# Layer norm, causal attention and a gated expert block: expert product in two pieces, four buffers for h, and another rule for the first score visits

## The chip, the cores and the metric

The kernel runs on one core of one Trainium2 chip. The metric is the device time of one execution in microseconds (us); less is better. Five engines work beside each other: TensorE (PE in the rows, its weight loads PEld), VectorE (DVE), ScalarE (ACT), GpSimd (POOL) and SyncE (SP), which here only issues DMAs. Each engine runs its own list of instructions in order and waits on semaphores for the others.

## The reference

For each of 8 sequences of 512 tokens with 128 channels (everything float32):

```
x = x + attn(layernorm(x))     # 16 heads of 8 channels, causal softmax, w_qkv, w_proj
x = x + experts(layernorm(x))

def experts(x):                # x: tokens x 128
    p = sigmoid(x @ Wg + bg)                      # 8 gates for each token
    weights = p * (p > 0.5)
    h = relu(einsum('td,edh->eth', x, W1) + b1)   # 8 experts, 512 hidden
    y = einsum('eth,ehd->etd', h, W2) + b2
    return einsum('te,etd->td', weights, y)
```

`layernorm` takes off the mean and multiplies by 1/sqrt(variance + 1e-5), without a scale or an offset.

## The kernel before

**Tiling.** A sequence lies with its 128 channels on the partitions and its 512 tokens along the row. The hidden layer of all experts is 4096 wide, which gives 32 slots of 128 for a sequence, four for each expert. A product of float32 accuracy is made of three matmuls in a faster form, from a high and a low part of each operand: `z` (slot s of x·W1) is L1107 to L1109, `y` (slot s of h·W2, added up in `y_bank` over the four slots of an expert) is L1293, L1295 and L1297. Between them ScalarE makes `h_hi` with a relu (L863), and the low part `h_lo` is made by VectorE straight from the bank (L1070, 20 slots of 32) or by GpSimd from a copy `h_all` (L869, L762, 12 slots). `h_hi` and `h_lo` are rings of three buffers. VectorE multiplies a finished expert by its gate (`term`, L1083), GpSimd adds it up (`acc`, L772). The gates are computed once for a sequence, written to memory (`gout`, L662) and read back, spread over all partitions, by one DMA for each expert (`wb`, L669) into four buffers.

**Attention.** Four groups of four heads. For a group there are 10 "max" units (scores with queries on the partitions; VectorE takes the row maxima, `smax`, L1018) and 10 "ex" units (scores with keys on the partitions and the maximum already taken off; ScalarE takes the exponential, L831). The scores come from `stack`, which holds the high and low parts of q and k interleaved: three DMAs for a group from `parts` (L641), and a fourth inside `stack` (L644). The maxima go GpSimd, TensorE (`nm`, L1238), ScalarE (L819) and SyncE (`mrow`, L655: two DMAs) back into `stack`. A *visit* of TensorE (L1166, with the causal mask added by L1178 for max units) takes two max units, or two ex units, or two of each side by side. GpSimd zeroes what is masked (`causal`, L755), and `pv` (L1248, 32 matmuls) multiplies by v.

**Layer norm.** VectorE takes statistics (L901, L905), GpSimd makes rstd (L713, L716), and VectorE normalises with four `tensor_scalar` instructions of 128x128 (L910), for `xT` (first norm) and `x2T` (second norm). Both write the buffer `xn`.

**What sets the order.** `list_schedule` makes the list of every engine before the program is built. Every item (`put` in `work_items`) has a due time, a cost in ns and the items it waits for; `SHIFT` moves the due times of a kind, for the first sequence (True) and for the others (False). An engine that falls idle takes the ready item with the earliest due time. `visits()` fixes the pairs of the score visits beforehand: the ex units follow the max units at a lag of 18 units until unit 50, and 12 from then on. TensorE has seven banks (`ring`), and `y_bank` as an eighth until the second norm of the first sequence (`EARLY_RING`). As long as there are eight, TensorE issues a dummy matmul (`warm`, L1193, result unused) when something is ready and cannot start. The item `("pe", ("y", i, s))` waits for `h_lo` of its slot; its first two matmuls read only `h_hi`.

**The start.** SyncE issues the loads of x, W1, the small weights and the third x, then the stack DMAs. The load of the third x (L630) waits for `x_bp` (GpSimd, L723), and this for the last of the small loads. VectorE first clears `stack` (L878, L879) and `nm` (L880). In the trace the masks are made at 3.1 us, the first transposes of TensorE start at 10.3, its matmuls on the small weights end at 18.35, and the first visit starts at 23.12.

## Time and profile before

| | |
|---|---|
| three runs | 685.42, 686.25, 686.25 us (median 686.25) |
| the profiled execution | 686.17 us, of it a span of 684.4 us |
| TensorE busy | 650.2 us, 95% of the span |
| VectorE, ScalarE, GpSimd busy | 480.8, 418.6, 330.9 us (70, 61, 48%) |
| mean granted clock of TensorE | 0.989 of full speed |
| by slices of 17.1 us, TensorE | 2 tenths, then 7, then 9 to the last slice (6) |

The span is what lies between the first and the last instruction of the profile; 1.8 us of the execution lie around it. A matmul is counted as busy until its result has landed, and the next starts before that; so the time that a matmul costs is read from the starts of two neighbours.

### The profile page before, as it was taken

How to read it: one execution, taken by the hardware profiler on the slowest of the kernel's cores; microseconds unless marked ns; L12 is line 12 of the kernel's file. 1: busy time of each engine (PE TensorE's matmuls, PEld its weight loads, DVE VectorE, ACT ScalarE, POOL GpSimd, SP SyncE). 2: the span in 40 equal slices, each digit the busy share in tenths (PEclk: the TensorE clock that was granted, in tenths of full speed). 3: DMA queues.
4: the chain of work that ended last, by engine and by line, in shares of the span. 5: the costliest groups of instructions: out<-in, count | busy, mean ns of one | idle time of the engine just before them, and what ended most of it. 6: DMA issues, size and time to landing. Idle time of an engine off the chain costs nothing.

```text
span 684.4 us, 13158 instructions
## 1 busy us (share of the span) xinstructions
PE 650.2 (95%) x4486; PEld 449.4 (66%) x4486; DVE 480.8 (70%) x958; ACT 418.6 (61%) x793; POOL 330.9 (48%) x409
## 2 busy tenths in 40 slices
PE   2799999999999989999999989999999999999996
PEld 2355666667666766667666756667666766677774
DVE  5797687679876796669866696668866676546443
ACT  2158656667666666676666566666666666665553
POOL 4018434556435454556335555455245564545554
PEclk9799999999999999999999999999999999999998
DMA  6442213210322113210222113220222102100310
GB/s 191 111 125 52 51 42 104 57 42 17 87 73 57 41 26 108 69 42 18 86 63 54 40 39 106 57 56 3 59 87 57 42 2 80 48 17 6 103 32 16
DMA packets 29954, 40.44 MB, mean 59 GB/s; under 512 B 4064, under 2 KB 14184, under 8 KB 29888
## 3 DMA queue, kind: packets, MB, share of 16 engines
q1 hardware_dynamic: 29360, 39.40, 21.4%
q8 instruction: 37, 0.61, 0.3%
q10 hardware_dynamic: 528, 0.20, 0.1%
q14 instruction: 29, 0.24, 0.1%
HBM read 23.72 MB, written 2.23 MB: 38 GB/s over the span
## 4 chain that ended last, share of the span: by engine, by line
PE 85%; DVE 6%; issue 3%; DMA 2%; SPq 2%; POOL 1%; ACT 1%; POOLq 0%; DVEq 0%
PE ring L1166 11%; PE ring L1248 10%; PE ring L1107 9%; PE ring L1109 9%; PE ring L1108 9%; PE y_bank L1293 8%; PE y_bank L1297 8%; PE y_bank L1295 8%; PE ring L1178 6%; PE ring L1113 3%; DVE xn L910 2%; PE ring L1193 2%; DVE negmax L1018 1%; DMA g_w<-in_L_ffn_b 1%; PE ring L1228 1%
## 5 line engine op out<-in xcount | busy, mean ns | idle before, releaser
L863 ACT ACTIVATE h_hi<-ring 128x512 fp32r<-128x512 f32 x256 | 153.4, 599 | 126.2 <-PE ring L1109 110.2
L831 ACT ACTIVATE pt<-ring 128x512 f32<-128x512 f32 x313 | 172.0, 596 | 54.7 <-PE ring L1166 51.8
L762 POOL TENSOR_TENSOR h_lo<-h_all,h_hi 128x512 fp32r<-128x512 f32 x96 | 123.9, 1290 | 149.5 <-ACT h_all L869 149.0
L1018 DVE TENSOR_REDUCE negmax<-ring 128x1 f32<-128x512 f32 (+1 forms) x185 | 119.2, 683 | 74.3 <-PE ring L1178 74.2
L1070 DVE SCALAR_TENSOR_TENSOR h_lo<-ring,h_hi 128x512 fp32r<-128x512 f32 x160 | 109.5, 686 | 56.0 <-ACT h_hi L863 52.7
L755 POOL TENSOR_SCALAR_AFFINE_SELECT pt<-pt 128x512 f32<-128x512 f32 x128 | 80.1, 640 | 110.9 <-ACT pt L831 110.8
L1293 PE MATMUL y_bank<-h_hi,w_lo 128*128 128x512 f32 x256 | 109.0, 426 | 1.1 <-DVE f_buf L1083 0.5
L1107 PE MATMUL ring<-x2T_lo,w_hi 128*128 128x512 f32 x256 | 108.0, 422 | 0.3 <-DVE negmax L1018 0.3
L1166 PE MATMUL ring<-stack 32*128 32x256 f32 (+3 forms) x992 | 94.9, 363 | 8.7 <-DMA stack<-stack 4.8
L1297 PE MATMUL y_bank<-h_lo,w_hi 128*128 128x512 f32 x256 | 100.6, 393 | 0.0
L1109 PE MATMUL ring<-x2T_hi,w_hi 128*128 128x512 f32 x256 | 100.5, 393 | 0.0
L1295 PE MATMUL y_bank<-h_hi,w_hi 128*128 128x512 f32 x256 | 99.9, 390 | 0.0
L1108 PE MATMUL ring<-x2T_hi,w_lo 128*128 128x512 f32 x256 | 99.9, 390 | 0.0
L1166 PEld LDWEIGHTS ring<-stack 32*128 32x128 f32 x992 | 55.4, 183 | 61.3 <-issue 55.3
L1018 DVE TENSOR_REDUCE pm<-ring 128x4 f32<-128x512 f32 x123 | 80.7, 681 | 13.0 <-PE ring L1178 12.2
L772 POOL TENSOR_TENSOR f_buf<-f_buf 128x512 f32<-128x512 f32 x56 | 72.2, 1290 | 21.2 <-DVE f_buf L1083 21.2
L1248 PE MATMUL ring<-pt,v_sb 128*32 128x512 f32 (+3 forms) x1024 | 75.5, 436 | 0.0
L1083 DVE SCALAR_TENSOR_TENSOR f_buf<-y_bank,b_cols,f_buf 128x512 f32<-128x512 f32 x64 | 47.9, 748 | 21.5 <-PE y_bank L1297 21.3
L1248 PEld LDWEIGHTS ring<-pt,v_sb 128*32 128x32 f32 x1024 | 30.0, 109 | 47.7 <-issue 42.1
L869 ACT ACTIVATE h_all<-ring 128x512 f32<-128x512 f32 x96 | 56.9, 592 | 0.0
L1293 PEld LDWEIGHTS y_bank<-h_hi,w_lo 128*128 128x128 f32 x256 | 48.2, 188 | 11.9 <-issue 2.0
L1178 PE MATMUL ring<-mask,ident 128*128 128x128 bf16 (+1 forms) x308 | 55.3, 258 | 0.0
(119 smaller groups left out, 754.1 us busy)
## 6 DMA issues: line engine op xcount, KB each, us to landing
f_buf<-gates SPq DMA_DIRECT2D x64, 256.0 KB, 3.3
stack<-parts SPq DMA_DIRECT2D x96, 128.0 KB
x_in<-in_L_attn_x SPq DMA_DIRECT2D x8, 256.0 KB, 2.9
f_buf<-in_L_ffn_W SPq DMA_DIRECT2D x1, 2048.0 KB, 10.4
out_x<-f_buf SPq DMA_DIRECT2D x8, 256.0 KB, 2.3
stack<-nmT SPq DMA_DIRECT2D x64, 8.0 KB
stack<-stack SPq DMA_DIRECT2D x32, 16.0 KB
bv<-in_L_attn_b_qkv SPq DMA_DIRECT2D x1, 256.0 KB
```

Of the source, the lines that this page charges most:

```text
L762: g_.tensor_tensor(h_lo[:, (i * SLOTS + s) % 3, :], h_all[:], h_hi[:, (i * SLOTS + s) % 3, :].bitcast(F32), ALU.subtract).then_inc(s_hlo_p ...
L831: sc.activation(pt[:, slot, :], b[:], ACT.Exp, scale=SCALE).then_inc(free_sem("ex", i, g, u), 1)
L863: sc.activation(h_hi[:, (i * SLOTS + s) % 3, :], bank_of("z", i, s)[:], ACT.Relu).then_inc(s_hhi, 1)
L1018: v.tensor_reduce(dst, src, AX.X, ALU.max, negate=True).then_inc(free_sem("max", i, g, u), 1)
L1107: mm(dst, hi, x_lo, start=True, stop=False)
L1108: mm(dst, lo, x_hi, start=False, stop=False)
L1109: return mm(dst, hi, x_hi, start=False, stop=True)
L1166: last = mm(out_, lhsT, rhs, start=(k == 0), stop=stop, skip_group_check=True)
L1248: last = mm(b[32 * j:32 * j + 32, kb * P:], v_sb[:, kb, g * GH + j, :], pt[:, slot, col:col + T - kb * P], start=(kb == 0 and g % 2 == 0), ...
L1293: mm(y_bank[:], w2_lo[:, s * C:(s + 1) * C], h_hi[:, (i * SLOTS + s) % 3, :], start=(s % HC == 0), stop=False)
L1295: mm(y_bank[:], w2_hi[:, s * C:(s + 1) * C], h_hi[:, (i * SLOTS + s) % 3, :], start=False, stop=False)
L1297: mm(y_bank[:], w2_hi[:, s * C:(s + 1) * C], h_lo[:, (i * SLOTS + s) % 3, :], start=False, stop=(s % HC == HC - 1)).then_inc(s_y, 1)
```

## The change

The instructions stay the same but for a few; what changes is mostly when each is issued.

- **y in two items.** `y` keeps the two matmuls that read `h_hi` and waits for `h_hi` alone; the third, which reads `h_lo`, becomes an item of its own, `ylo`, with the wait for `h_lo`.
- **h four deep.** `h_hi` and `h_lo` are rings of four (`H_RING`). To make room, `center` lies in `oT`.
- **Layer norm.** The normalise instructions become `scalar_tensor_tensor`, with rstd as a second tensor, spread with step 0.
- **Visits.** The list of `visits()` is gone. While there are eight banks, `next_visit` takes max units or ex units alone when only these are ready, with a lag of up to 26; later it keeps the lag of 12. `FFN_LAG` is 59 for 54, and `SHIFT` has other numbers.
- **Gates.** One DMA brings the gates of two experts (512 KB) into two buffers.
- **Dummies.** They are also issued when nothing is ready for TensorE, from the moment the masks are made.
- **The start.** VectorE's clearing of `stack` is two items of the order, the second behind the first norm. The DMA inside `stack` is left out for the first sequence, and the third DMA of its first group is issued by ScalarE.

```diff
+H_RING = 4
-HEAD_LAG, HEAD_UNITS = 18, 50
-FFN_LAG = 54
+HEAD_LAG = 26
+FFN_LAG = 59
...
-         ('dve', 'ln2n', False): 8.5,
+         ('dve', 'ln2n', False): 13.0,
...
+    put("dve", ("stackset", 0), -40, 1765)
+    put("dve", ("stackset", 1), -18.5, 1900, ("dve", ("ln1n", 0)))
+    put("act", ("stack", 0), -17, 100, ("dve", ("klo", 0)), ("dve", ("stackset", 1)))
...
-            put("act", ("hhi", i, s), f0 + s + .2, 600, ("pe", ("z", i, s)), ("pe", ("y", f3, s3)))
+            put("act", ("hhi", i, s), f0 + s + .2, 600, ("pe", ("z", i, s)), ("pe", ("ylo", f3, s3)))
...
-            put("pe", ("y", i, s), f0 + s + 1.9, 690,
-                ("pool" if s in POOL_SPLITS else "dve", ("hlo", i, s)),
-                ("pe", ("y", *divmod(i * SLOTS + s - 1, SLOTS))),
+            put("pe", ("y", i, s), f0 + s + 1.9, 460, ("act", ("hhi", i, s)),
                 ("dve", ("term", *divmod((i * SLOTS + s) // HC - 1, EXPERTS))))
+            put("pe", ("ylo", i, s), f0 + s + 2.2, 230, ("pe", ("y", i, s)),
+                ("pool" if s in POOL_SPLITS else "dve", ("hlo", i, s)))
...
+    def next_visit(free):
+
+
+        mx, ex = ([(kind, *n) for n in units[begun[kind]:begun[kind] + 2]] for kind in ("max", "ex"))
+        lag = begun["max"] - begun["ex"]
+        ready_now = [bool(pair) and all(("pe", unit) in ready["pe"] for unit in pair)
+                     for pair in (mx, ex)]
+        if banks == EARLY_RING:
+            if not ready_now[0] or lag >= HEAD_LAG or (ready_now[1] and free < 4):
+                mx = []
+            if not ready_now[1]:
+                ex = []
+            return (mx, ex) if free >= len(mx) + len(ex) else ([], [])
+        if lag > EXP_LAG:
+            mx = []
+        elif lag < EXP_LAG and mx:
+            ex = []
+        wanted = [ok for pair, ok in zip((mx, ex), ready_now) if pair]
+        return (mx, ex) if all(wanted) and free >= len(mx) + len(ex) else ([], [])
...
-            if idle[engine] and ready[engine]:
-                if engine == "pe":
-                    pick_pe(now)
-                else:
-                    start(now, engine, min(ready[engine], key=lambda key: work[key][0]))
+            if engine == "pe" and idle[engine]:
+                pick_pe(now)
+            elif idle[engine] and ready[engine]:
+                start(now, engine, min(ready[engine], key=lambda key: work[key][0]))
...
-                    for s, (a, b) in enumerate(zip(Q_PART, K_PART)):
-                        sp.dma_start(rows[s::4, :, :, :],
-                                     parts[32 * g:32 * g + 32, a:3 + b:2 + b - a, :].bitcast(F32)
-                                     ).then_inc(s_stack[g], 16)
-                    sp.dma_start(rows[M_ROW::M_STEP, :, 0, :],
-                                 rows[M_ROW + 4::M_STEP, :, 0, :]).then_inc(s_stack[g], 16)
+                    for s in range(3 if i or g else 2):
+                        sp.dma_start(rows[s::4, :, :, :], halves(g, s)).then_inc(s_stack[g], 16)
+                    if i:
+                        sp.dma_start(rows[M_ROW::M_STEP, :, 0, :],
+                                     rows[M_ROW + 4::M_STEP, :, 0, :]).then_inc(s_stack[g], 16)
...
-                    wait(sp, s_term, i * EXPERTS + e - 3)
-                    sp.dma_start(wb[:, e % 4, :], gates_dram[e:e + 1].broadcast_to([P, T])
-                                 ).then_inc(s_wb[e % 4], 16)
+                    wait(sp, s_term, i * EXPERTS + e - 2)
+                    sp.dma_start(wb[:, e % 4:e % 4 + 2, :],
+                                 gates_dram[e:e + 2].rearrange("(a e) t -> a e t", a=1)
+                                 .broadcast_to([P, 2, T])).then_inc(s_wb[e // 2 % 2], 16)
...
-                        v.tensor_scalar(dst[:, t, :], src[:, t, :], mv[:, n, t, 0:1],
-                                        rstd[:, n, t:t + 1], ALU.subtract,
-                                        ALU.mult).then_inc(done, 1)
+                        v.scalar_tensor_tensor(out=dst[:, t, :], in0=src[:, t, :],
+                                               scalar=mv[:, n, t, 0:1],
+                                               in1=rstd[:, n, t:t + 1].broadcast_to([P, C]),
+                                               op0=ALU.subtract, op1=ALU.mult).then_inc(done, 1)
...
-                    wait_split(pe, i, s)
+                    pe.wait_ge(s_hhi, i * SLOTS + s + 1)
...
+                elif kind == "ylo":
+                    s = w[2]
+                    wait_split(pe, i, s)
+                    mm(y_bank[:], w2_hi[:, s * C:(s + 1) * C], h_lo[:, (i * SLOTS + s) % H_RING, :],
+                       start=False, stop=(s % HC == HC - 1), skip_group_check=True).then_inc(s_y, 1)
```

TensorE's list at the very start, before: the transposes of the first norm (`xn`), then k, q and v, the small weights and the first visit.

```order
L1113 MATMUL ring<-ident,xn 128x128 x4
L1107 MATMUL ring<-xT_lo,wqk_hi 128x512
L1108 MATMUL ring<-xT_hi,wqk_lo 128x512
L1109 MATMUL ring<-xT_hi,wqk_hi 128x512
...
L1228 MATMUL ring<-wqkv_in,xT 128x128 x4
L1204 MATMUL ring<-ident,g_w 128x8
L1205 MATMUL ring<-wg_in,center 128x8
L1166 MATMUL ring<-stack 128x512 x2
```

The same place in the changed kernel (its dummies have L1233, the transposes L1153, the visit L1206).

```order
L1233 MATMUL ring<-mask,ident 128x256 x53
L1153 MATMUL ring<-ident,xn 128x128 x4
L1233 MATMUL ring<-mask,ident 128x256 x19
L1147 MATMUL ring<-xT_lo,wqk_hi 128x512
...
L1268 MATMUL ring<-wqkv_in,xT 128x128 x4
L1244 MATMUL ring<-ident,g_w 128x8
L1245 MATMUL ring<-wg_in,oT 128x8
L1233 MATMUL ring<-mask,ident 128x256 x18
L1206 MATMUL ring<-stack 128x512 x2
```

53, 19 and 18 dummies, 90 in all, now stand ahead of the first visit, and 46 behind it; before, all 131 stood behind it. The visits are 188 for 169: 132 with both kinds for 151, 28 with max units alone for 9, and 28 with ex units alone for 9.

TensorE's list around the second norm of the fourth sequence (`x2T`, the lower `ident,xn` row), before: `nm`, then `xT`, a slot of z, a slot of y, and `x2T`.

```order
L1297 MATMUL y_bank<-h_lo,w_hi 128x512
L1238 MATMUL ring<-ident,nm 128x128
L1113 MATMUL ring<-ident,xn 128x128 x4
L1107 MATMUL ring<-x2T_lo,w_hi 128x512
L1108 MATMUL ring<-x2T_hi,w_lo 128x512
L1109 MATMUL ring<-x2T_hi,w_hi 128x512
L1293 MATMUL y_bank<-h_hi,w_lo 128x512
L1295 MATMUL y_bank<-h_hi,w_hi 128x512
L1297 MATMUL y_bank<-h_lo,w_hi 128x512
L1113 MATMUL ring<-ident,xn 128x128 x4
```

The same place in the changed kernel, from one slot earlier: `x2T` (L1153) stands right behind `nm` (L1278), and `xT` of the sixth sequence is already done some 45 rows earlier.

```order
L1333 MATMUL y_bank<-h_hi,w_lo 128x512
L1335 MATMUL y_bank<-h_hi,w_hi 128x512
L1147 MATMUL ring<-x2T_lo,w_hi 128x512
L1148 MATMUL ring<-x2T_hi,w_lo 128x512
L1149 MATMUL ring<-x2T_hi,w_hi 128x512
L1340 MATMUL y_bank<-h_lo,w_hi 128x512
L1206 MATMUL ring<-stack 128x512 x2
L1206 MATMUL ring<-stack 128x256 x4
L1218 MATMUL ring<-mask,ident 128x128 x2
L1278 MATMUL ring<-ident,nm 128x128
L1153 MATMUL ring<-ident,xn 128x128 x4
```

The low part of a slot (L1340) now stands behind the next slot of z. VectorE has the four normalise instructions ahead of the maxima of that last visit, where before two maxima stood in front of them.

## Rows read from the trace of the kernel before

**Rows 1.** Stretches: length, then busy of PE, PEld, DVE, ACT, POOL; PEclk, DMA, GB/s.
```profile
23.12:31.20 8.08, 8.08 (x26) 3.73 (x26) 5.11 (x10) 0.60 (x1) 0.00 (x0) 0.50 0.60 137
31.20:54.00 22.80, 21.96 (x145) 12.78 (x145) 21.91 (x53) 12.00 (x24) 4.64 (x10) 1.00 0.35 95
54.00:100.50 46.50, 45.40 (x461) 29.16 (x457) 33.32 (x82) 31.14 (x63) 25.15 (x37) 1.00 0.23 53
100.50:674.80 574.30, 564.90 (x3827) 396.52 (x3825) 403.16 (x781) 370.51 (x701) 289.18 (x341) 1.00 0.19 53
```

**Rows 2.** What PE waited for, 60 us to the end: us in total, times, longest.
```profile
PE ring L1113 <- DVE xn L910: 5.5, 5, 1.3
```

**Rows 3.** In order of time, 16 to 24 us: start us, us, instruction, idle before it.
```profile
18.12 0.38 SPq L630 DMA_DIRECT2D x_in<-in_L_attn_x  x1
...
18.61 1.98 SPq L641 DMA_DIRECT2D stack<-parts  x3
...
20.63 0.61 SPq L644 DMA_DIRECT2D stack<-stack  x1
...
23.12 0.79 PE L1166 MATMUL ring<-stack 32*128 32x512 f32 x2 [4.77 <-DMA stack<-stack]
```

**Rows 4.** PE in order of time, 76 to 82 us: dummies and visits.
```profile
76.69 0.50 PE L1166 MATMUL ring<-stack 32*128 32x384 f32 x4
77.12 0.50 PE L1193 MATMUL ring<-mask,ident 128*128 128x256 bf16 x3
...
78.26 1.48 PE L1193 MATMUL ring<-mask,ident 128*128 128x256 bf16 x12
79.68 0.50 PE L1166 MATMUL ring<-stack 32*128 32x512 f32 x2
...
80.23 1.04 PE L1193 MATMUL ring<-mask,ident 128*128 128x256 bf16 x8
81.20 0.50 PE L1166 MATMUL ring<-stack 32*128 32x384 f32 x6
```

**Rows 5.** PE, 61 to 63 us: a visit with both kinds.
```profile
61.36 0.79 PE L1166 MATMUL ring<-stack 32*128 32x384 f32 x8
...
62.31 0.82 PE L1193 MATMUL ring<-mask,ident 128*128 128x256 bf16 x6
```

**Rows 6.** PE, 31.5 to 32.5 us: a visit of max units alone.
```profile
31.65 0.50 PE L1166 MATMUL ring<-stack 32*128 32x256 f32 x4
...
32.32 0.38 PE L1211 MATMUL ring<-g_w,x 72*128 72x512 bf16 x1
```

**Rows 7.** PE, DVE and POOL, 319 to 325 us: second norm of the fourth sequence.
```profile
319.63 0.29 PE L1178 MATMUL ring<-mask,ident 128*128 128x128 bf16 x2
...
319.90 1.29 DVE L1018 TENSOR_REDUCE negmax<-ring 128x1 f32<-128x512 f32 x2
...
321.21 2.48 DVE L910 TENSOR_SCALAR xn<-x,mv,rstd 128x128 f32<-128x128 f32 x4
321.22 1.29 POOL L762 TENSOR_TENSOR h_lo<-h_all,h_hi 128x512 fp32r<-128x512 f32 x1
...
321.47 0.40 PE L1109 MATMUL ring<-x2T_hi,w_hi 128*128 128x512 f32 x1
321.70 0.40 PE L1293 MATMUL y_bank<-h_hi,w_lo 128*128 128x512 f32 x1
...
323.83 0.63 PE L1113 MATMUL ring<-ident,xn 128*128 128x128 f32 x4 [1.28 <-DVE xn L910]
```

**Rows 8.** DVE lines: ns min/median/max of one, first and last start us.
```profile
L910 DVE TENSOR_SCALAR xn<-x,mv,rstd x32: 332/338/1379, 94.8 to 619.5; 128x128 f32<-128x128 f32 x32
L1063 DVE SCALAR_TENSOR_TENSOR g_w<-g_tanh,g_w x8: 678/680/1662, 103.6 to 628.4; 8x512 f32<-8x512 f32 x8
```

**Rows 9.** PEld at the end of the last expert, in order of time.
```profile
676.61 0.19 PEld L1293 LDWEIGHTS y_bank<-h_hi,w_lo 128*128 128x128 f32 x1 [0.54 <-DVE h_lo L1070]
```

**Rows 10.** The gate DMAs (L669), issue to landing.
```profile
DMA to landing us min/median/max: 3.0/3.3/4.8
```

More of the change, by code:

```diff
@@ L99 @@
[L99 to L114 removed]
+         ('pool', 'nm', True): -16.0}
@@ L296, in list_schedule @@
     form = "full"
-    masks_made = False
-    score_visits = visits()
+    units = [(i, g, u) for i in range(BATCH) for g in range(GROUPS) for u in range(N_U)]
+    begun = {"max": 0, "ex": 0}
     def at(time, what, key):
@@ L325, in start @@
             form = new
-            if item[0] != "y":
+            if item[0] not in ("y", "ylo"):
                 fill(item)
@@ L371, in pick_pe @@
                 continue
-            if item[0] != "y" and not free:
+            if item[0] not in ("y", "ylo") and not free:
                 continue
@@ L382, in pick_pe @@
             best = pv
[L383 to L392 removed]
+        mx, ex = next_visit(free)
+        if mx or ex:
+            due = min(work[("pe", unit)][0] for unit in (*mx, *ex))
+            due += SWITCH_DUE if form == "full" else 0
+            if best is None or due < best[0]:
+                if pv and form == "full" and free + item_odd(pv) > len(mx) + len(ex):
+                    start(now, "pe", pv[1])
                     return
+                begun["max"] += len(mx)
+                begun["ex"] += len(ex)
+                start_scores(now, mx, ex)
+                return
         if best is not None:
@@ L425, in list_schedule @@
                 emptied_at[emptier[key]] = now
-            if key == ("pool", ("mask", None)):
+            if what == "done" and key == ("pool", ("mask", None)):
                 masks_made = True
```

163 lines of the change are left out of this document (81 added, 82 removed).

## The prediction, written before the changed kernel had run

> **What bounds the kernel now.** I read the stretches first. After the experts have begun (100.5 us), TensorE is busy 564.9 of 574.3 us [rows 1]: the reader is to see that this stretch is worth hardly more than its 9.4 us of idle time, since the matmuls themselves stay the same. Ahead of it lie 77.4 us (23.12 to 100.5) in which TensorE is counted as busy too, but there the busy time hides two things: 8.08 us at a granted clock of 0.50, and dummies. Then the waits of TensorE: of the 9.4 us, 5.5 are waits for the normalised xn, five times, up to 1.3 us [rows 2]. Last, the start in order of time: TensorE stands still 4.77 us in front of its first visit at 23.12, for the stack DMAs [rows 3]. So the time is: the first visit, plus what TensorE has to issue behind it at its clock, plus a dozen us of waits, plus the last chain. I go through the change by these.
>
> The sum is made against the profiled execution, 686.17 us (span 684.4); that is 0.08 us below the median of the runs, so the two can be taken as one.
>
> **The first visit.** SyncE issues the third x at 18.12, and the first stack DMA at 18.61; three take 1.98 us, 0.66 each, the fourth is issued at 20.63 and TensorE starts 2.49 us later [rows 3]. In the changed order the load of x is still ahead of them and still waits for x_bp, so 18.61 stays, however early q and k are ready. Two DMAs are left on SyncE, the third goes out on ScalarE meanwhile, and the one inside stack is gone. The last is issued at 18.61 + 0.66 = 19.27, and the first visit starts at 19.27 + 2.49 = 21.76: −1.4 us. Bounds: 0, if three DMAs side by side land as late as four in a row, and −2.0 (three issues saved). ScalarE's issue has nothing queued behind it that could start so early.
>
> **The clock.** Before the first visit TensorE is idle for 4.8 us, and from 23.12 to 31.20 the granted clock is 0.50, which is 1.2 GHz; TensorE is busy all of it [rows 1]. The 18 dummies that now stand between the small weights and the first visit keep it busy for some 2 of these us, and it comes out of 72 more. If it then starts at 2.4 GHz, TensorE's work of that stretch takes 4.04 instead of 8.08 us. But VectorE is the next limit: over 23.12 to 54 it is busy 5.11 + 21.91 = 27.0 of 30.9 us [rows 1], and the clearing of v_sb now falls into this stretch as well. So 3.9 us is the most that can be had before VectorE has no gap left, and some is had back behind 54 us, where it has 13 us free. I take −3.0; bounds −4.0 and 0 (the clock falls all the same).
>
> **Dummies and visits.** A dummy costs 0.11 us: 12 of them fill 78.26 to 79.68, 8 fill 80.23 to 81.20, and the difference is 0.45 for four; what is left over, 0.09, is the switch into a visit [rows 4]. Behind the first visit there are 131 now and 46 in the changed kernel: −85 × 0.11 = −9.3 us. The 90 ahead of it cost nothing as long as they end before xT, q and k are wanted. If the first 53 all ran at half the clock they would take 53 × 0.22 = 11.7 us from 3.1 us on, and the first transposes (10.3 us now) would start at 14.8; the cover is the 18.61 of SyncE and the faster products behind. It is thin: without it the first visit would be late by what is over.
>
> Against that stand 19 visits more. A visit of max units alone takes 0.67 us [rows 6], one of ex units alone 0.43 (76.69 to 77.12), one with both 0.55 (79.68 to 80.23) [rows 4] to 0.95 [rows 5], by whether the two kinds fall into the same rows of the array; I take the middle, 0.75. Splitting one costs 0.67 + 0.43 − 0.75 = 0.35 and at most one more switch of 0.09: 19 × 0.44 = 8.4 us. So this big exchange comes to −0.9 us. Its bounds are −5 and +3 (with 0.95 or 0.55 for the visit of both). What it really does is fill with work the places that dummies held, and begin the experts with 72 max units done for 66.
>
> **The second norm.** From the masks of the visit (319.63) to the point at which TensorE wanted x2T (323.83 − 1.28 = 322.55) there are 2.9 us. VectorE needs 0.27 to start, 1.29 for two maxima, 2.48 for the four normalise instructions and 0.1 to hand over: 4.2, hence the wait of 1.28 [rows 7]. The order now puts the normalise behind the maxima of the visit before. TensorE has behind that visit a low part, z, two matmuls of y, z, a low part, another visit and nm: ten matmuls of 0.23 (the step in rows 7), 0.75 + 0.2 and 0.1 and the 0.15 of the masks, 3.5 us. VectorE needs 0.27 + 1.29 + 0.1 and the four instructions. For these the row of before has 338 ns in the middle and 1379 at most; two-tensor instructions of 512 elements take 680 ns [rows 8]. So one of 128 lies between 170 and 338 ns; I take 250, which is 0.35 less for four. With the collision of before that is 2.13, together 3.8: a wait of 0.3 is left of 1.28, five times. −4.0 us with some lost elsewhere; bounds −5.5 and 0. Behind the first norm no one waits but in the head, where it is covered.
>
> The long ones among the normalise instructions lie beside GpSimd's: at 321.21 one starts as GpSimd starts its h_lo (321.22, 1.29), and the four take 2.48 [rows 7]. The two-tensor form is not free of this: the one that the kernel already has takes 680 ns and once 1662 [rows 8]. The Trainium skill says the same ("SBUF — State Buffer", section "Who interferes with whom"): a VectorE instruction with two inputs in SBUF contends with a GpSimd instruction that reads SBUF, and the second to issue waits for the whole of the first. Going by that rule I leave the collision in the sum; had the new form been free of it, the wait would be gone and the sum 1 us lower.
>
> **y in two items, h four deep.** The matmuls are the same. The step from the last of z to the first of y is 0.23 us, as inside an item [rows 7], so 256 item borders more cost 0; at most one hundredth each, 2.6 us. What they take away is small as well: of the 9.4 us idle behind the first z, at most the 3.9 that are not xn's [rows 1, 2], and I count none of it. At the end the last h_lo is waited for 0.54 us with three matmuls behind it [rows 9]; now only one is, which is 2 × 0.23 = −0.5 us.
>
> **The gates in pairs.** 32 DMA issues fewer on SyncE, which nobody waits for: 0. A pair is wanted three experts ahead, and a single one lands after 3.3 us [rows 10]. What is queued behind it is a rival below. center in oT costs nothing: it is read for the last time long before the first oT is written.
>
> **Sum.** −1.4 − 3.0 − 0.9 − 4.0 − 0.5 = −9.8 us; 686.2 − 9.8 = 676.4 us.
>
> **Rivals.** *The clock falls again.* Between the last of the 18 dummies and the first visit TensorE is idle for up to 2.7 us (they end at 19 if the small weights come as now, and 21.76 is the visit). In the profile of before it had been idle for 4.8 us. Then the 3.0 are lost: 679.4 us. For it speaks that the dummies are counted out beforehand, against it that the idle time is about half. The Trainium skill ("TensorE: Matmul & The Clock Gate", section "What's actually happening") adds that the chip looks in windows that run free of the kernel, so by it the same gap could cost the clock in one run and not in another; the runs would then lie apart by these 3 us.
> *The wait for x2T stays.* It does, if GpSimd's instructions collide with all four normalise instructions, or rstd comes late because the order now asks for it earlier. The 4.0 are lost: 680.4 us. For it: the place is earlier by one visit also for GpSimd; against it: 1.0 us more of slack by count.
> *VectorE is the bound of the head.* Then the earlier visits only wait for free banks, nothing is gained from the clock or the first visit, and the split visits cost their 8.4 less what the dummies give: with half of the 9.3 not recovered the loss is 4.7, and −4.5 for norm and end remain: about 686, no change. Against it: 33.3 of 46.5 us behind 54 us [rows 1].
> *The pairs hold up the maxima (slower than before).* The two DMAs that bring the maxima into stack stand in the same queue of SyncE behind the pairs, and a pair is issued only when the expert three before it is finished, one expert later than now. The maxima need two issues of 0.66 and, if they land as the stack DMAs do, 2.49 us [rows 3], with ScalarE's copy some 4 us; TensorE's list has some 5 us of other items in between. Behind a pair (3.3 us for half of one [rows 10], so up to 3.3 more) they are late from the point at which this adds over 1 us; at the full 3.3 it is 2.3 us for one group in each of the last 6 sequences, 13.8 us: 690 us. Against it: no wait for the maxima stands among the largest of TensorE behind 60 us, and the queues are seldom full (DMA share 0.19 [rows 1]).
>
> **How the numbers follow.** Forecast 676.4, between 672.5 and 680, 60%. The clock falls, 679.4: 17%. x2T stays, 680.4: 10%. VectorE bounds the head, no change: 5%. The pairs, slower: 8%. For 8 in 10 the range takes in the first three and the lower bounds of the dummies and the norm together: 670.5 to 683. Faster by over 0.2% (below 684.9; 0.2% is about what a measurement of this kernel can tell from no change): 0.87, within it 0.05, slower 0.08.
>
> **What would show it.** First visit at 21.8 us and not 23.1; granted clock 1.0 from there on; dummies behind it over 5 us and not 14; the first z at 96 us or a little before; waits of TensorE for xn under 2 us behind 60 us; idle of TensorE behind the first z about 5 us. It is wrong if the first visit comes after 23, if a clock of 0.50 follows it, or if new waits for smax banks, for stack<-nmT or for f_buf<-gates stand in the waits of TensorE with more than 3 us in all.

## The result, and the profile after

The changed kernel takes 693.73 us (median of 4 runs, 692.66 to 695.63), the kernel before 685.84 (684.76 to 686.25): ratio 1.012, 95% interval 1.010 to 1.015. The forecast was 676.4 us (670.5 to 683.0); the time went the other way, 17.3 us above it. The profiled execution of the changed kernel took 695.63 us, with a span of 694.1 and a mean granted clock of 0.977 (0.989 before).

First two lines of the page of the changed kernel: TensorE busy and granted clock, in 40 slices of 17.4 us.

```profile
PE   7799899999999999999999999999999999998996
...
PEclk9899599999999999999999999999999999999998
```

The fifth slice (69 to 87 us) has a granted clock of five tenths while TensorE is counted as busy for eight tenths of it. Nothing like it stands in the profile of before. The stretches of the changed kernel, with the columns of [rows 1]:

```profile
24.05:30.42 6.37, 6.37 (x22) 2.90 (x23) 3.68 (x6) 0.60 (x1) 0.00 (x0) 0.50 0.62 142
30.42:69.81 39.39, 37.53 (x269) 19.53 (x267) 38.25 (x86) 24.32 (x48) 15.14 (x25) 1.00 0.30 77
71.38:88.45 17.07, 15.63 (x81) 6.86 (x83) 9.10 (x19) 4.40 (x9) 6.08 (x9) 0.50 0.11 25
88.45:111.28 22.83, 21.83 (x202) 13.35 (x203) 17.75 (x45) 16.55 (x34) 8.54 (x16) 1.00 0.21 51
111.28:628.35 517.07, 512.57 (x3576) 355.23 (x3576) 389.80 (x734) 341.05 (x646) 264.44 (x316) 1.00 0.18 54
631.17:634.58 3.41, 3.41 (x11) 2.65 (x10) 0.69 (x1) 1.68 (x3) 0.00 (x0) 0.50 0.00 0
```

Three things are to be seen. TensorE works at a clock of 0.50 (1.2 GHz) in three stretches of together 26.85 us, against one of 8.08 before [rows 1] (in both kernels the clock is low once more in the last 5 us, behind the experts, which is left out here); if all that work is bound by TensorE, 13.4 us are lost against 4.0, and the difference, 9.4, is nearly the 9.7 us by which the span grew. From 30 to 70 us VectorE is busy 38.25 of 39.39 us. And the experts begin later: the gate matmuls of the first sequence, which now stand just ahead of the first z, come at 111.28; before, the first z came at 100.5.

What TensorE waited for in the changed kernel (us in total, times, longest):

```profile
PE ring L1206 <- DMA stack<-parts: 3.7, 1, 3.7
PE ring L1147 <- DVE h_lo L1110: 3.5, 6, 0.6
PE ring L1206 <- DVE negmax L1058: 3.2, 2, 3.0
...
PE ring L1153 <- DVE xn L944: 2.3, 1, 2.3
```

The five waits of 1.3 us for xn [rows 2] are gone, as forecast. In their place stand six of 0.6 us at a z and one of 2.3 us for the last second norm; and in the head there is one of 3.0 us for a bank. That last one in order of time, TensorE first:

```profile
69.32 0.50 PE L1206 MATMUL ring<-stack 32*128 32x384 f32 x4
72.82 0.79 PE L1206 MATMUL ring<-stack 32*128 32x384 f32 x4 [3.00 <-DVE negmax L1058]
```

VectorE at the same place:

```profile
68.08 4.09 DVE L944 SCALAR_TENSOR_TENSOR xn<-x_in,mv,rstd 128x128 f32<-128x128 f32 x4
72.09 0.68 DVE L1058 TENSOR_REDUCE negmax<-ring 128x1 f32<-128x512 f32 x1
```

And GpSimd:

```profile
67.56 3.81 POOL L761 TENSOR_TENSOR w_lo<-f_buf,w_hi 128x512 fp32r<-128x512 f32 x3
71.34 0.68 POOL L788 TENSOR_SCALAR_AFFINE_SELECT pt<-pt 128x512 f32<-128x512 f32 x1
```

VectorE's four normalise instructions for the third sequence took 4.09 us, because GpSimd ran three splits of w2 (67.56 to 71.37) beside them. The first sequence's four, with no such split beside them, took 1.17 us. The maximum behind them is what frees the bank, so TensorE stood still from 69.81 to 72.82, and in that time, at 71.38, its clock fell. It stayed at 0.50 for 17.07 us.

### The profile page after: what moved, and what is told of

Same layout as the page of the kernel before. It is cut to its first block, busy times and chain, and to the rows that moved or that the text cites. A ratio compares the mean times of both kernels' runs of the same rounds, so it can differ in the third digit from the quotient of the medians.

```text
span 694.1 us, 13093 instructions
## 1 busy us (share of the span) xinstructions
PE 665.0 (96%) x4491; PEld 453.9 (65%) x4491; DVE 501.8 (72%) x958; ACT 420.6 (61%) x793; POOL 335.2 (48%) x409
## 4 chain that ended last, share of the span: by engine, by line
PE 85%; DVE 6%; issue 4%; DMA 2%; SPq 1%; POOL 1%; ACT 0%; POOLq 0%; DVEq 0%
PE ring L1206 11%; PE ring L1288 11%; PE ring L1147 9%; PE y_bank L1333 8%; PE ring L1148 8%; PE ring L1149 8%; PE y_bank L1340 8%; PE y_bank L1335 8%; PE ring L1218 6%; PE ring L1153 3%; DMA g_w<-in_L_ffn_b 1%; DVE xn L944 1%; DVE negmax L1058 1%; PE ring L1304 1%; PE ring L1268 1%
## 5 line engine op out<-in xcount | busy, mean ns | idle before, releaser
L869 ACT ACTIVATE pt<-ring 128x512 f32<-128x512 f32 x315 | 177.1, 600 | 55.1 <-PE ring L1206 53.8
L788 POOL TENSOR_SCALAR_AFFINE_SELECT pt<-pt 128x512 f32<-128x512 f32 x128 | 83.2, 663 | 69.6 <-ACT pt L869 69.5
L1206 PE MATMUL ring<-stack 32*128 32x128 f32 (+2 forms) x998 | 103.6, 370 | 8.7 <-DMA stack<-parts 3.7
L1147 PE MATMUL ring<-x2T_lo,w_hi 128*128 128x512 f32 x256 | 102.8, 402 | 3.5 <-DVE h_lo L1110 3.5
L1149 PE MATMUL ring<-x2T_hi,w_hi 128*128 128x512 f32 x256 | 100.5, 393 | 0.0
L1058 DVE TENSOR_REDUCE pm<-ring 128x4 f32<-128x512 f32 x124 | 80.2, 682 | 26.8 <-PE ring L1218 26.8
L1206 PEld LDWEIGHTS ring<-stack 32*128 32x128 f32 x998 | 58.3, 186 | 62.9 <-issue 55.0
L1340 PE MATMUL y_bank<-h_lo,w_hi 128*128 128x512 f32 x256 | 97.4, 409 | 0.0
L805 POOL TENSOR_TENSOR f_buf<-f_buf 128x512 f32<-128x512 f32 x56 | 73.9, 1319 | 11.7 <-DVE f_buf L1123 11.7
L1288 PE MATMUL ring<-pt,v_sb 128*32 128x512 f32 (+3 forms) x1024 | 77.7, 445 | 0.0
L1147 PEld LDWEIGHTS ring<-x2T_lo,w_hi 128*128 128x128 f32 x256 | 48.5, 189 | 15.3 <-DVE h_lo L1110 6.5
L1333 PEld LDWEIGHTS y_bank<-h_hi,w_lo 128*128 128x128 f32 x256 | 48.4, 189 | 13.8 <-ACT h_hi L901 4.5
```

What stands on the lines that cost most here:

```text
L869: sc.activation(pt[:, slot, :], b[:], ACT.Exp, scale=SCALE).then_inc(free_sem("ex", i, g, u), 1)
L1058: v.tensor_reduce(dst, src, AX.X, ALU.max, negate=True).then_inc(free_sem("max", i, g, u), 1)
L1147: mm(dst, hi, x_lo, start=True, stop=False)
L1149: return mm(dst, hi, x_hi, start=False, stop=True)
L1206: last = mm(out_, lhsT, rhs, start=(k == 0), stop=stop, skip_group_check=True)
L1288: last = mm(b[32 * j:32 * j + 32, kb * P:], v_sb[:, kb, g * GH + j, :], pt[:, slot, col:col + T - kb * P], start=(kb == 0 and g % 2 == 0), ...
```

## The experiments

Two theories stood against each other. **Clock**: the changed kernel loses by the falls of the clock, and they come from idle time and from the dummies that are no longer there. **VectorE**: the head is bound by VectorE, and the clock only slows what would wait anyway. Ratios are to the kernel before, of runs on the same chip; its medians there were 685.0 to 685.6 us. A dummy is the `warm` item; edits to the order are made on the finished list.

### The stall and the clock

**fill_71** puts 26 dummies into the stall, and leaves it as it is.

```diff
+ORDER["pe"][177:177] = [("warm", 1, 9)] * 26
```

> The changed kernel with 26 more dummy matmuls of 0.11 us each, put in front of the visit that waits from 69.81 to 72.82 us: the wait stays as long as it is, TensorE only does something in it. Clock theory: granted clock 1.00 through 71.38 to 88.45, pv back from 4.4 to 2.3 us, 8.5 us less: about 685. Rival (VectorE bounds the head): the clock stays up and the time does not fall, 692 to 694, because waits take the place of the slower matmuls.

686.92 us (685.63 to 687.40), ratio 1.001 (1.000 to 1.002). 6.8 us of the loss come back from matmuls that compute nothing. The rows of 71.38 to 88.45 us, same columns as above:

```profile
71.38:88.45 17.07, 17.07 (x161) 9.26 (x160) 11.90 (x25) 9.67 (x21) 7.00 (x13) 1.00 0.22 51
```

161 matmuls stand where 81 stood, at a clock of 1.00. Not all of the 6.8 us need be the fall at 71: in the profiled execution the fall at the start lasted 3.41 us for 6.83 and the one at 631 did not come, while one of 3.41 us came at 103.

**w2_waits** takes the cause of the stall away instead.

```diff
                 elif kind == "w2":
                     pool.wait_ge(s_w2hi, i + 1)
+                    if i == 3:
+                        pool.wait_ge(s_xn, 3 * TB)
```

> The changed kernel with one wait added: GpSimd starts its run of w2 splits (the 3.81 us of them at 67.56 us) only when VectorE has normalised the third sequence. Clock theory: VectorE's four normalising instructions took 4.09 us there beside GpSimd against 1.17 us at 7.35 us without it; with 2.9 us less, the 3.00 us in which TensorE waits for a bank (69.81 to 72.82) go almost wholly, the half clock of 71.38 to 88.45 (17.07 us) does not come, and 8.5 us of lost speed go with it: 693.7 - 8.5 - 1.5 = about 684. Rival (VectorE, 97% busy from 30 to 71 us, is what makes the head long, and the low clock only fills time in which TensorE would wait): at most the 2.9 us of the stretched normalise come back, 691 to 693.

686.07 us, but with runs from 683.14 to 691.25, ratio 1.002 (0.999 to 1.005). The normalise took 1.12 us and the stall went:

```profile
67.53 1.12 DVE L946 SCALAR_TENSOR_TENSOR xn<-x_in,mv,rstd 128x128 f32<-128x128 f32 x4
```

Yet that did not decide the clock. The ten runs lie almost in order of their mean granted clock, 683.1 and 683.4 us at 0.994, 685.1 to 685.4 at 0.989 to 0.992, 686.8 and 687.4 at 0.987, 689.6 and 690.6 at 0.981 and 0.980, 691.3 at 0.977. In the profiled one (690.64 us) the clock fell all the same; the stretches ahead of the fall and behind it:

```profile
62.00:70.49 8.49, 7.96 (x74) 4.17 (x74) 8.46 (x19) 6.86 (x15) 5.93 (x8) 1.00 0.23 54
70.49:84.14 13.65, 13.65 (x74) 5.70 (x72) 6.91 (x13) 4.19 (x9) 7.87 (x11) 0.50 0.13 31
```

Ahead of this fall TensorE is counted as busy for 7.96 of 8.49 us, with no gap above 0.25 us: score visits and a pv, and hardly a dummy between. With the stall the mean clock was low in all four runs (0.977 to 0.982); without it, it is low in some and not in others. What decides between them is not shown.

**before_no_dummies** asks the same of the kernel before.

```diff
+ORDER["pe"] = [w for w in ORDER["pe"] if w[0] != "warm"]
```

> The kernel before without its 131 dummy matmuls (14.4 us of TensorE's time between 54 and 100 us), order otherwise unchanged. Clock theory: they are what kept the granted clock at 1.00 there, since without them idle stretches of 1 to 2 us follow one another; the clock falls at least once between 54 and 100 us and costs 5 to 15 us: 690 to 700. Rival (my prediction's term: dummies only delay real work, 0.11 us each where one is under way when an item gets ready): 676 to 686, no half clock between 31 and 679 us.

695.54 us (691.38 to 697.64), ratio 1.014 (1.010 to 1.018): 131 matmuls less, and 10 us more. The clock theory holds, the term of my prediction does not. Its stretches at half the clock (by the record, each fall begins 0.4 us inside its row):

```profile
46.22:59.88 13.66, 12.75 (x63) 6.96 (x64) 11.41 (x23) 9.12 (x17) 3.58 (x7) 0.51 0.35 96
...
66.70:73.53 6.83, 6.53 (x46) 2.29 (x45) 3.28 (x7) 2.39 (x5) 5.65 (x9) 0.53 0.26 61
...
87.18:90.60 3.42, 3.42 (x26) 0.91 (x24) 1.49 (x3) 1.39 (x3) 0.97 (x2) 0.56 0.54 120
...
100.84:107.66 6.82, 5.42 (x36) 2.29 (x36) 2.14 (x6) 0.00 (x0) 1.30 (x2) 0.53 0.42 101
```

All four come at or behind places where dummies stood. In the kernel before, the first dummy is issued at 43.14 us (not at 54, as I had it when I wrote what I expected), and 19 of them lie ahead of 46.2:

```profile
L1193 PE MATMUL ring<-mask,ident x110: 269/273/283, 43.1 to 95.0; 128*128 128x256 bf16 x110
```

Of the dummies alone, busy of PE and PEld:

```profile
23.12:46.20 23.08, 2.32 (x19) 1.69 (x20) 0.82 0.33 79
```

Without them TensorE waits 1.47 us for a bank there, and the first fall follows. The fall at the start is not in these rows, yet the first score matmuls (23.73 us) take 0.79 us as in the kernel before, and 0.49 with the clock held (before_fill_start): here the record of the clock seems to miss a fall, so a mean granted clock is a guide and not a measure.

**fill_all** adds 33 dummies ahead of the first visit and 20 ahead of the eighth sequence's second norm to the 26.

```diff
+ORDER["pe"][1138:1138] = [("warm", 2, 140)] * 20
+ORDER["pe"][177:177] = [("warm", 1, 9)] * 26
+ORDER["pe"][95:95] = ORDER["pe"][94:95] * 33
```

> The same 26 dummies, 33 more in front of the first visit (in the wait of 20.39 to 24.05 us) and 20 more in front of the eighth sequence's second-norm transposes (wait of 628.35 to 630.68 us). Clock theory: all three half-clock stretches of 6.83, 17.07 and 3.41 us go; with work in 6.37 + 17.07 + 3.41 = 26.85 us of them, half of it comes back, 13.4 us: about 680, below the kernel before (685.8). Rival: the first piece is bound by the stack's transfers and VectorE's maxima (3.4 us of the 13.4 don't come back): 684; with VectorE bounding all of the head only the 1.7 us of the last piece come back, 692.

685.32 us (683.84 to 685.74), ratio 0.9995 (0.9985 to 1.0005). The clock was held but for one stretch of 3.41 us, and 8.4 of the 13.4 us came back. The first rival (684) comes nearest: at full clock TensorE waits for others in part of these stretches.

**before_fill_start** gives the kernel before the same help, 42 dummies in front of its first visit.

```diff
+ORDER["pe"][5:5] = [("warm", *RING_USE[("max", 0, 0, 0)])] * 42
```

> The kernel before with 42 more dummy matmuls (4.6 us) in front of its first visit, where TensorE is idle from 18.34 to 23.12 us; nothing else changed. Clock theory: the half clock of 21.01 to 31.25 us, in which work ran for 8.1 us, does not come; half of these come back: 685.5 - 4 = 681.5. Rival (the first pieces are bound by VectorE's maxima and the transfers): the clock is held and the time stays, 684.5 to 685.5.

682.93 us (682.61 to 683.47), ratio 0.996 (0.995 to 0.998): −2.1 us where 4 were expected, faster than both kernels. Its stretch behind the first visit ran at 1.00, and there VectorE is the next limit, busy 7.24 of 7.87 us:

```profile
23.38:31.25 7.87, 7.87 (x41) 3.95 (x42) 7.24 (x16) 1.79 (x3) 0.18 (x1) 1.00 0.63 146
31.25:97.50 66.25, 64.20 (x588) 40.36 (x586) 53.51 (x129) 41.95 (x84) 29.62 (x47) 1.00 0.28 70
97.50:674.53 577.03, 567.87 (x3836) 398.00 (x3834) 404.09 (x782) 370.95 (x702) 290.02 (x341) 1.00 0.19 53
```

**waits_and_fills** joins the wait of w2_waits, the fills at 24 and 628 us, and 24 dummies spread over four places between 64 and 70 us. It is the changed kernel with its clock held but for 3.41 us at 99.7, and the base of what follows.

```diff
+ORDER["pe"][1138:1138] = [("warm", 2, 140)] * 20
+ORDER["pe"][177:177] = [("warm", 1, 9)] * 8
+ORDER["pe"][175:175] = [("warm", 2, 13)] * 4
+ORDER["pe"][173:173] = [("warm", 0, 10)] * 4
+ORDER["pe"][171:171] = [("warm", 7, 10)] * 8
+ORDER["pe"][95:95] = ORDER["pe"][94:95] * 33
```

> The changed kernel with GpSimd's w2 splits held back behind the third sequence's normalise (it alone gave 683.1 to 691.3 by run, with a mean granted clock of 0.994 to 0.977), 33 dummies before the first visit, 24 in four places between 64 and 70 us and 20 before the eighth sequence's second-norm transposes. Clock theory: granted clock 1.00 from the first visit to the tail in all runs and none of the 3.0 us stall: fill_all's 685.3 less 1 to 3 us, 682 to 684. Rival (VectorE, at 9.8 of 10 us busy from 30 to 70 us, bounds it): 685.

684.02 us (682.16 to 685.67), ratio 0.998 (0.996 to 0.999). From its first visit to its first z, and from there to the last y:

```profile
22.45:100.84 78.39, 75.61 (x599) 42.45 (x599) 69.00 (x159) 47.77 (x95) 32.24 (x53) 0.99 0.29 71
100.84:675.36 574.52, 568.23 (x3823) 398.80 (x3821) 415.63 (x768) 368.91 (x693) 291.74 (x336) 1.00 0.18 53
```

Against before_fill_start the head is 4.3 us longer (78.39 to 7.87 + 66.25 = 74.12) and the rest 2.5 shorter (574.52 to 577.03). VectorE's busy time in the head is 69.0 against 7.24 + 53.51 = 60.8 us. The two cuts are not quite the same: the three gate matmuls lie ahead of the first z here (1.27 us at half clock) and behind it there (0.70 us).

### The visits and the order table

**before_new_visits** is the kernel before with `next_visit` and its lag of 26 in place of `visits()`, **after_old_visits** the changed kernel with the reverse.

```diff
-HEAD_LAG, HEAD_UNITS = 18, 50
+HEAD_LAG = 26
...
-        if score_visits:
-            mx, ex = score_visits[0]
...
+        mx, ex = next_visit(free)
+        if mx or ex:
```

> The kernel before with only visits when ready (59 dummies are left of 131). Clock theory: the granted clock falls in the head once or more, 5 to 10 us lost, less the 0 to 3 us that earlier visits win: 688 to 695. Rival (first visits when ready are a gain, and what lost the time is elsewhere in the change): 679 to 685.

689.13 us (688.32 to 690.49), ratio 1.006 (1.004 to 1.008). The new rule alone loses 4 us, as the clock theory had it; its profile shows a clock of 0.50 in 52.9 to 59.7, 73.4 to 80.2 and 107.5 to 110.9 us, beside the fall at the start.

> The changed kernel with the visits of the kernel before (pairs of maxima and exponentials together, at most 18 units apart in the head) in place of visits when ready; all else of the change stays, the order table included. Clock theory: 226 dummies against 136, most of the 90 more between 50 and 110 us, hold the clock at 1.00 there, the head falls by 8 to 10 us and the rest keeps its gain of 2: 693.7 - 9 = about 684. Rival (VectorE bounds the head whatever the visits are): 688 to 693.

691.11 us (690.00 to 692.66), ratio 1.008 (1.006 to 1.011). The clock theory's 684 does not hold, though the clock stayed at 1.00 from 29 to 108 us. The time lies in the rival's range, but not for the rival's reason alone: VectorE is busy for 66.90 of the 78.40 us from 29.4 to 107.8. From first visit to first z it took 90.0 us, and gate and first z stand 12 us apart. That this is so because the order table was made for other visits is my reading; no run takes it apart.

**old_order_new_parts** therefore takes the table and the lag of before as well, and keeps the rest of the change (y in two items, h four deep, norm form, pairs, dummies from time zero).

```diff
-FFN_LAG = 59
+FFN_LAG = 54
...
+ORDER["pe"][95:95] = ORDER["pe"][94:95] * 33
...
```

> The changed kernel with the visits, the order table and the expert stage's lag of the kernel before, and 33 more dummies ahead of the first visit: so y in two items, h four deep, the two-tensor normalise, paired gates and dummies from time zero are in it, the order of the head is the old one. Clock theory: granted clock 1.00 from the first visit on, head as in before with 42 dummies (74 us, that kernel 682.9). The order theory (the gain in the rest lies in the expert term's two items and the deeper h): 2 to 4 us less than that, 679 to 681. Rival (the gain in the rest is the order table's): 682.5 to 684.

690.60 us (689.29 to 691.53), ratio 1.007 (1.005 to 1.009). Both expectations fail. The head is as expected, 74.25 us; the rest is 8.7 us longer than in before_fill_start (at most 1.7 of them from a fall of the clock of 3.41 us at 480), and the wait that the change was to remove has grown:

```profile
23.01:97.26 74.25, 72.09 (x629) 44.34 (x628) 60.33 (x144) 43.72 (x87) 29.73 (x47) 1.00 0.30 74
97.26:682.95 585.69, 571.80 (x3836) 395.53 (x3834) 402.64 (x782) 374.92 (x702) 290.57 (x341) 1.00 0.18 52
```

```profile
PE ring L1144 <- DVE xn L935: 8.1, 6, 2.0
```

So the parts are no gain under the old table. Which of them lengthens this stretch was not taken apart further.

### The parts by themselves, with the clock held and the order unchanged

**y_joined** issues the three matmuls of a slot where the third one stands.

```diff
                 elif kind == "y":
                     s = w[2]
+                    continue
+                elif kind == "ylo":
+                    s = w[2]
                     pe.wait_ge(s_hhi, i * SLOTS + s + 1)
+                    wait_split(pe, i, s)
...
-                elif kind == "ylo":
-                    s = w[2]
-                    wait_split(pe, i, s)
                     mm(y_bank[:], w2_hi[:, s * C:(s + 1) * C], h_lo[:, (i * SLOTS + s) % H_RING, :],
```

> The kernel waits_and_fills (684.0 us) with the three y matmuls of a slot together at the place of the third one, the order else the same. By my prediction's term (two items instead of one: nothing), 684 to 685. Rival (the two-item form is what lets the waits of 1.25 us for normalised x, 5 in the kernel before, and those for h_lo be filled): the time rises by 3 us or more, with PE waiting for h_lo.

690.12 us (688.73 to 690.44), +6.1 us. Its stretch from first z to last y is 580.65 us against 574.52. The two items are worth 6 us under this table; I had them at nothing. The same stretch as in the base:

```profile
101.70:682.35 580.65, 570.96 (x3823) 399.89 (x3821) 412.08 (x768) 362.02 (x693) 292.09 (x336) 1.00 0.18 52
```

3.4 us of the difference are idle time (9.69 for 6.29), and 2.7 lie between matmuls that are counted as busy; no single wait is long.

**one_tensor_norm** goes back to `tensor_scalar`, **gates_singly** to one DMA for each gate.

```diff
-                        v.scalar_tensor_tensor(out=dst[:, t, :], in0=src[:, t, :],
...
+                        v.tensor_scalar(dst[:, t, :], src[:, t, :], mv[:, n, t, 0:1],
```

```diff
+                    for n in (e, e + 1):
+                        sp.dma_start(wb[:, n % 4, :], gates_dram[n:n + 1].broadcast_to([P, T])
+                                     ).then_inc(s_wb[e // 2 % 2], 16)
...
```

> waits_and_fills with VectorE's normalise in the form of the kernel before (one tensor, two scalars a row), the order the same. Both forms took about the same alone (340 and 346 ns) and beside GpSimd (up to 1379 and 1384 ns): 683.5 to 684.5. Rival (the two-tensor form suffers more beside GpSimd): 1 to 4 us faster.

> waits_and_fills with each gate row broadcast by a transfer of its own (64 of 256 KB) in place of 32 of two rows; waits and buffers the same. By my prediction's term (pairs cost nothing and bring nothing): 683.5 to 684.5. Rival (the pair transfers hold up the stack's and the terms): 1 us or more faster.

681.95 us (681.28 to 682.75), ratio 0.995 (0.993 to 0.996), and 682.32 us (682.00 to 683.29), ratio 0.996 (0.994 to 0.997), where the base had 0.998 (0.996 to 0.999). Both come out nearer to their rivals; the difference of the first (0.0031) is larger than its uncertainty (0.0020), that of the second (0.0021) hardly is. With both undone (**norm_and_gates_old**)

> waits_and_fills with both the normalise in the form of the kernel before and the gate rows sent singly. If each is worth what its run said (682.0 and 682.3 against 684.0): 680.2 to 681. If these two were the chip's scatter: 682 to 684.

it was 681.30 us (681.04 to 683.72), ratio 0.995 (0.993 to 0.997). Its median is 2.7 us below the base, its ratio 0.0026 (1.8 us) with an uncertainty of 0.0023. So the two cost about 2 us together (0.2 to 3.4), they don't add up, and how it divides stays open.

### Is VectorE the bound of the head?

Each of the ten maxima of the first sequence's third group is taken twice, in both kernels.

```diff
+                    if (i, g) == (0, 2):
+                        n = 4 if qb == 20 else len(heads) == 2 and 2 or 1
+                        v.tensor_reduce(twice[:, u, 0:n], src, AX.X, ALU.max, negate=True)
                     v.tensor_reduce(dst, src, AX.X, ALU.max,
```

> before_fill_start (682.9 us) with the same 10 maxima taken twice. If VectorE bounds the head of the kernel before as well: 5 to 6 us longer, 688 to 689; if the visits by the old rule bound it: 0 to 2 us.

> waits_and_fills (684.0 us) in which VectorE takes each of the 10 maxima of the third head group of the first sequence twice (the second result is not used): 10 more instructions of 0.60 us, 6.0 us of VectorE's time between 45 and 65 us. If VectorE (9.6 to 10 us of each 10 us busy from 30 to 70 us) bounds the head: 5 to 6 us longer, 689 to 690. If TensorE does, whose dummies can give way: 0 to 2 us longer.

In the kernel before it took 688.55 us (688.43 to 690.13) after 682.93: +5.6 for 6.0 us of VectorE. Nor is that the clock alone: its four runs have mean granted clocks of 0.996, 0.993, 0.992 and 0.991, and the one with 0.996, as in before_fill_start, took 688.55 as well. In the changed one 692.26 us (690.01 to 695.56) after 684.02: +8.2. VectorE bounds a stretch of the head in both. And where it makes TensorE wait, the clock falls on top, here for 20.48 us in the changed kernel:

```profile
53.13:73.61 20.48, 19.77 (x90) 11.26 (x94) 17.23 (x40) 10.83 (x21) 8.55 (x14) 0.50 0.18 42
```

and for 6.83 us in the one before:

```profile
51.85:58.67 6.82, 6.41 (x28) 2.89 (x31) 6.82 (x14) 3.67 (x7) 1.02 (x3) 0.50 0.00 0
```

The two runs of twice_max_after with a mean granted clock of 0.993 took 690.0 and 690.4 us (+6.2), those with 0.981 and 0.989 took 695.6 and 694.1.

### What took the place of the wait for xn

In norm_and_gates_old, at the end of a sequence, VectorE in order of time:

```profile
250.24 1.06 DVE L1107 TENSOR_SCALAR g_w<-g_tanh 8x512 f32<-8x512 f32 x1
251.34 1.67 DVE L1110 SCALAR_TENSOR_TENSOR g_w<-g_tanh,g_w 8x512 f32<-8x512 f32 x1
252.94 0.67 DVE L1117 SCALAR_TENSOR_TENSOR h_lo<-ring,h_hi 128x512 fp32r<-128x512 f32 x1
```

GpSimd:

```profile
249.74 1.28 POOL L803 TENSOR_TENSOR h_lo<-h_all,h_hi 128x512 fp32r<-128x512 f32 x1
250.97 1.49 POOL L813 TENSOR_TENSOR f_buf<-f_buf 128x512 f32<-128x512 f32 x1
```

TensorE:

```profile
252.67 0.39 PE L1342 MATMUL y_bank<-h_hi,w_hi 128*128 128x512 f32 x1
253.66 0.50 PE L1154 MATMUL ring<-x2T_lo,w_hi 128*128 128x512 f32 x1 [0.60 <-DVE h_lo L1117]
```

The z at 253.66 needs the bank that h_lo frees; h_lo had its `h_hi` since 251 and stood behind the two gate instructions, which took 2.7 us beside GpSimd. The gates are not wanted for a long time yet. **gate_behind_hlo** swaps the two items in the order of VectorE.

```diff
+for n in range(1, 7):
+    at = ORDER["dve"].index(("gate", n))
+    ORDER["dve"][at:at + 2] = ORDER["dve"][at:at + 2][::-1]
```

> norm_and_gates_old with VectorE's two gate instructions (1.06 and 1.67 us beside GpSimd) behind the h_lo that stands after them, for sequences 1 to 6. The z that waits 0.60 us for that h_lo, 6 times, should not wait: 3 to 3.6 us less than that kernel. Rival: the h_lo after it is late instead, by as much: no difference.

677.07 us (675.81 to 677.52), ratio 0.988 (0.987 to 0.989): −4.2 us against norm_and_gates_old, and the fastest version here, 7.9 us below the kernel before on the same chip and below the changed one by 16.7. VectorE at the same place:

```profile
249.73 0.69 DVE L1120 SCALAR_TENSOR_TENSOR h_lo<-ring,h_hi 128x512 fp32r<-128x512 f32 x1 [0.57 <-ACT h_hi L912]
250.34 1.06 DVE L1110 TENSOR_SCALAR g_w<-g_tanh 8x512 f32<-8x512 f32 x1
251.43 1.00 DVE L1113 SCALAR_TENSOR_TENSOR g_w<-g_tanh,g_w 8x512 f32<-8x512 f32 x1
```

And the stretch from its first z to its last y:

```profile
100.47:667.69 567.22, 564.77 (x3823) 398.88 (x3821) 411.50 (x769) 368.86 (x694) 287.98 (x337) 1.00 0.19 54
```

2.45 us of idle time are left in 567.2. The kernel before has 9.51 in 577.08 between the same two points (the row in [rows 1] ends 2.8 us ahead of the last y):

```profile
100.50:677.58 577.08, 567.57 (x3836) 398.10 (x3834) 404.19 (x782) 371.11 (x702) 290.41 (x341) 1.00 0.19 53
```

The second gate instruction also got shorter, 1.00 for 1.67 us; it now starts elsewhere against GpSimd's.

## Why the prediction was wrong, by its own steps

**Dummies and visits (−0.9): the step that failed.** I priced a dummy at 0.11 us of TensorE and nothing else, and so counted 85 fewer as 9.3 us won. What they do is hold the clock: without them the kernel before loses 10 us, and 26 more in the right place give the changed kernel 6.8 back. Nor was the time they filled TensorE's to win. VectorE bounds the head, so what dummies give up is filled by waiting. The 8.4 us for split visits were not far off: from start to start, waits taken off, the matmuls on `stack` in the head take 25.6 us (210) in waits_and_fills and 19.0 (188) in before_fill_start, those of the masks 8.5 and 6.9; of this difference of 8.2 some 2 belong to the 12 units done earlier, which leaves 6. I had the rows for it, VectorE at 21.91 of 22.80 us [rows 1], and used them against the clock's gain only.

**The clock (−3.0).** The half clock at the start did not go: 18 dummies, then 3.66 us idle, then 0.50 from 23.59 to 30.42. That was my first rival, at 17%. Held up by dummies, it is worth 2.1 us in the kernel before; the term was too large by VectorE's share. What no rival of mine held is that the clock could fall where it had been steady. It did, at 71.38 and at 631.17, each time in or right behind a wait of TensorE (3.00 and 2.33 us). Of the 17.3 us between forecast and result, fill_71 gives 6.8 back, most of them by the fall at 71, and fill_all 1.6 more. The other 8.9 are gains that I had counted here and below and that did not come; gate_behind_hlo, without the new norm form and the pairs and with the swap, is 8.2 us below fill_all.

**The first visit (−1.4).** It came at 24.05, 0.9 later. I held 18.61 for the first stack DMA fixed; it was issued at 20.01, because the third x ahead of it (19.52) waited for x_bp, which GpSimd began at 17.89 instead of 16.76 when its small load had landed later. The last of SyncE's two stack DMAs then went out at 20.67, and TensorE started 3.4 us behind it and not 2.49. Over the profiled executions the first visit lies at 22.45 to 24.05 in the changed order and at 22.64 to 23.73 in the old one: nothing won that can be measured.

**The second norm (−4.0).** The waits for xn went, as worked out. But I asked only whether the normalise would be early enough, not what it would push back: the order now has a z waiting 0.6 us, six times, for an h_lo behind the gates, and one norm at the end that waits 2.33. In waits_and_fills the rest is 2.5 us shorter than in before_fill_start, and some of that is work that moved into the head. With the swap, and norm form and gates as before, it is 9.8 us shorter (567.22 for 577.03): the gain was there, one place further on.

**y in two items and h four deep (0, and −0.5 at the end).** The two items are worth 6.1 us under this order; my bound was that at most 3.9 us of idle time were to be had. The bound was wrong because the table around them had changed: undone, they cost new waits. Of the 0.5 at the end at most 0.3 were to be had: before_fill_start steps 0.49 us where the last h_lo is waited for (673.08 to 673.57), against 0.23. I did not try h three deep.

**Norm form and pairs (0 each).** Together they cost about 2 us. The rival of the pairs (maxima late, 13.8 us) did not come: no wait for stack<-nmT stands in the waits of the changed kernel's TensorE. My 250 ns for the two-tensor form was wrong as well: alone it takes 337 ns at least, `tensor_scalar` 332 [rows 8]. Beside GpSimd both are stretched, to 1384 ns and to 1379 [rows 8]. The Trainium skill names a way into that contention for each ("SBUF — State Buffer", section "Who interferes with whom"): two inputs in SBUF, and for tensor_scalar the two-port mode that it can enter. The trace agrees that both are stretched: four two-tensor instructions took 4.09 us beside GpSimd's splits and 1.12 without them (w2_waits). The line of the changed kernel (ns min/median/max of one, first and last start us):

```profile
L944 DVE SCALAR_TENSOR_TENSOR xn<-x_in,mv,rstd x32: 337/346/1384, 7.3 to 403.8; 128x128 f32<-128x128 f32 x32
```

**The rival that came nearest** is "VectorE is the bound of the head, about 686", to which I gave 5%. That is what the changed kernel is with the clock held (684.0 to 685.3). The falls of the clock come on top.

**What would show it.** Of my signs the first already told: a first visit after 23, and a clock of 0.50 behind it.

## What to carry to other kernels

Matmuls that compute nothing are not idle time to be reclaimed: before counting them as a gain, ask what the granted clock does without them, and price each new wait of TensorE in a sparse stretch at the work that follows at half speed, not at its own length. Where an engine beside TensorE is busy for over nine tenths of a stretch, expect little from work saved on TensorE there. And when an order is re-planned to remove a wait, look one item further on the same queue: here two small instructions, wanted much later, stood ahead of the one that frees a bank, and swapping them gave 4.2 us.

## What the runs showed of the hardware

The clock can fall without a gap: at about 70.5 us in w2_waits, with TensorE counted as busy 7.96 of the 8.49 us ahead and no gap above 0.25 us. The Trainium skill ("TensorE: Matmul & The Clock Gate", section "What's actually happening") ties the low state to idle time; here it fell behind score visits and pv, matmuls of 32 rows or 32 columns that are counted as busy, and not in every run. So one and the same kernel took 683.1 to 691.3 us, in step with its mean granted clock. The kernel before has two levels as well, 684.4 to 685.1 us at a mean clock of 0.993 to 0.999 and 685.4 to 686.5 at 0.989 (14 runs).

It also came back late. In the changed kernel TensorE is counted as busy for 15.63 of the 17.07 us at 0.50 behind its 3 us stall, in twice_max_after for 19.77 of 20.48, while behind the shorter wait at 628 us, with the dense matmuls of the experts, the low clock lasted 3.41 us.

A wait of 2.3 us for the last second norm was followed by a fall in the changed kernel (2.33 us from 628.35), and in fill_71, at the same place in the order, by none:

```profile
622.76 0.63 PE L1154 MATMUL ring<-ident,xn 128*128 128x128 f32 x4 [2.31 <-DVE xn L945]
```

So the length of a single wait doesn't decide it.
